# Batched table loads in the edge walks of a graph-attention kernel

## The chip, the cores and the metric

The kernel runs on one core of one Trainium2 chip. The metric is the device time of one execution in microseconds (us), as the median of several runs; lower is better. The profile is one further execution, recorded by the hardware profiler.

## The reference

The kernel computes one block of a graph network over 6250 nodes with 256 features and 200,000 edges sorted by their destination node. Two graph-attention layers come first (four heads of 128 features, then one head of 256), beside a linear-attention mix, and after them a mixture of eight expert networks. What the walks below compute is the attention:

```python
h = (x @ W).reshape(n, heads, out_ch)
logits = leaky_relu(al_s[src] + al_d[dst], 0.2)
m = segment_max(logits, dst)
e = exp(logits - m[dst])
denom = segment_sum(e, dst)
out = segment_sum(h[src] * (e / denom[dst])[:, :, None], dst)
```

For every edge the features of the source node are fetched, weighted, and summed into the destination node. Self loops are added apart from the walks.

## The kernel before, in words

One program runs these stages in order: a first pass (normalised input, `h` for layer 1, and tables over the edges written to HBM), walk 1 (layer 1, `H` = 4 heads in `A` = 2 halves), a finish of layer 1, walk 2 (layer 2, `H` = 1, with the linear-attention mix worked in between), a finish of layer 2, and the experts. Both walks are the same function, `walk_pass` (line 562).

A walk goes over 83 chunks (`CHUNKS`) of ten steps (`CS`), each step two tiles (`TPS`) of 128 edges, so 20 tiles (`CT`) a chunk. The loops over chunks are plain Python loops: every chunk's instructions stand in the program one after the other, and `TURN` with `i`, `r` only numbers slots and semaphore counts. What each engine does in a chunk c:

- POOL (`gather`, L861) issues 20 indirect DMAs that fetch the rows of the source nodes of chunk c into a ring of `RS` chunks (2 in walk 1, 3 in walk 2). Before each step it waits until the same step of the chunk `RS` earlier has been multiplied, and before each chunk until the index table of the chunk is in (`index_in`).
- ACT (`weights` L876 and L878, `scale` L886) takes the exponentials and multiplies three of the four heads' rows by their weights; DVE (`scale`, L1235) does the fourth head in walk 1.
- PE (`multiply`, L1022) sums the weighted rows of a step into at most 128 destination nodes ("a window") by a one-hot matrix `hit`. After step 0 it also runs `spread_targets` for chunk c+1 (L919, twenty small matmuls, which raise `spread_out`); after steps 3 to 6 come four small turns for chunk c+1 (L926, L931, L932, L937, L938, L1007).
- DVE builds `hit` (L1219, from the table `meta`), adds each step's sum into the window's accumulator (L1243 to L1252; the window's number is read into a register by `windows_of`, L713, from the table `win`), and between the steps works out the softmax maxima of chunk c+1: `terms` (L1164 to L1174), `scan_tiles` (L1179, L1180), `scan_ends`, `scan_through` (L1194 to L1200), `gaps` (L1205 to L1214), which raises `gap_ready`, and then `hits_turned` for chunk c+2 (L1160).
- SP only issues DMAs. Its part for chunk c is `follow`, in this order: wait until `gaps` of chunk c is done (this falls at step 6 of chunk c-1), then `load_resets` of chunk c+2 (L775, one DMA for each head, then L777 and L778); wait until all sums of chunk c-1 are added, then `load_tables` of chunk c+2 (`meta` L758, `win` L759) and `load_index` of chunk c+5 (L755); wait for `spread_out` of chunk c+1, then `load_places` of chunk c+2 (L762, 640 KB); then `load_goals` of chunk c+2: wait for its tables (L767), read ten window numbers into registers (L713), and issue ten small DMAs (L770) that PE's `spread_targets` of chunk c+2 waits for.

`index` has six slots (`TS`), `meta` and `win` three (`IS`), `resets` two. Every slot of `index` and of the tables has a semaphore of its own. A slot of `win` is `WROW` = 12 words wide, for ten numbers. At the start of a walk SP loads the index tables of five chunks and the other tables of two, then the places of chunk 0; after a wait for DVE's `cleared` it loads the resets of two chunks and the first goals.

Of the kernel before, what the change touches and what calls it, by code (L numbers as in the profile page):

```python
# [10 lines left out]
ALU = mybir.AluOpType  # L11
# [6 lines left out]
P = 128  # L18
# [23 lines left out]
W = P  # L42
# [4 lines left out]
CS = 10  # L47
CT = CS * TPS
CHUNKS = -(-STEPS // CS)
TURN = 6  # L50
GROUP = 4
CGROUPS = CT // GROUP
BLOCK_ROW = 2 * TPS * P + 2
# [56 lines left out]
def after(engine, sem, n):  # L110

    engine.wait_ge(sem, n + 1)
# [7 lines left out]
def spread(ap, axis, n):  # L120

    shape = list(ap.shape)
    return ap.unsqueeze(axis).to_broadcast(shape[:axis] + [n] + shape[axis:])
# [438 lines left out]
def walk_pass(nc, k, d, layer, H, A, F, attn, acc, table):  # L562
# [3 lines left out]
    HP = H // A  # L566
# [2 lines left out]
    WIDE = OUT + HP  # L569
    RS = 2 if H > 1 else 3  # L570
    TS = 6
    IS = 3
    WROW = -(-CS // 4) * 4
    HA = H - 1 if H > 1 else H
    RK = H * (CT + 1)
    SPREAD = 3 * 2 * H
# [2 lines left out]
    HBUF = 3  # L579
    assert CHUNKS * CS >= STEPS and CHUNKS * CS <= SP  # L580
    assert TURN % RS == 0 and TURN % TS == 0 and TURN % IS == 0 and TURN * CS % PBUF == 0 and TURN * CGROUPS % HBUF == 0
    with ExitStack() as ctx:
        m = Memory(nc, ctx, f"walk{layer}")
        ring = m.sb("ring", [P, RS, CT, A * HALF_ROW])
        index = m.sb("index", [P, TS, CT], I32)
        meta = m.sb("meta", [P, IS, 2, CT])
        win = m.sb("win", [1, IS, WROW], I32)
        hitT = m.sb("hitT", [W, CT * P], BF16)
        target = m.sb("target", [P, NT, 3, 2 * H], BF16)
        goal = m.sb("goal", [P, CS, 3, 2 * H], BF16)  # L590
        resets = m.sb("resets", [RK, 2, 2, P])
# [13 lines left out]
        hit = m.sb("hit", [P, HBUF, GROUP, W])  # L605
# [59 lines left out]
        count = pK[:, 0:W]  # L665
        weight_k = pK[:, W:W + CT]

        index_in = [m.sem(f"index_in{r}") for r in range(TS)]
        tables_in = [m.sem(f"tables_in{r}") for r in range(IS)]
        place_in = m.sem("place_in")  # L670
        goals_in = m.sem("goals_in")
        resets_in = [m.sem("resets_in0"), m.sem("resets_in1")]
# [24 lines left out]
        def loop(body):  # L697

            def run(eng):
                for c in range(CHUNKS):  # L700
                    body(c, c // TURN, c % TURN)

            return run

        def after_this(c, i, r):

            if c == CHUNKS - 1:
                return None
            return (c + 1, i + (r + 1) // TURN, (r + 1) % TURN)

        def windows_of(engine, r):

            return nc.values_load_multi_w_load_instructions(win[0:1, r % IS, 0:CS], engines=[engine], min_val=0, max_val=NW - 1,  # L713
                                                              skip_runtime_bounds_check_because="a group's number is a count over NW - 1 comparisons")[1]
# [10 lines left out]
        def rows_of(i, r):  # L725

            return (i * (TURN // RS) + r // RS + 1) * (16 * CT)

        def resets_of(i, r):

            return (i * (TURN // 2) + r // 2 + 1) * (16 * (H + 2))

        def index_of(i, r):

            return (i * (TURN // TS) + r // TS + 1) * 16

        def tables_of(i, r):

            return (i * (TURN // IS) + r // IS + 1) * 32

# [9 lines left out]
        with nc.Block() as block:  # L750

            @block.sync
            def _(sp):
                def load_index(c, r):
                    sp.dma_start(index[:, r % TS, :], d["index"][:, bass.ds(c * CT, CT)]).then_inc(index_in[r % TS], 16)  # L755

                def load_tables(c, r):
                    sp.dma_start(meta[:, r % IS, :, :], d["meta"][:, :, bass.ds(c * CT, CT)]).then_inc(tables_in[r % IS], 16)  # L758
                    sp.dma_start(win[:, r % IS, 0:CS], d["windows"].unsqueeze(0)[:, bass.ds(c * CS, CS)]).then_inc(tables_in[r % IS], 16)  # L759

                def load_places(n):
                    sp.dma_start(hitT[:, :], d["places"][0:CHUNKS * CS, :].rearrange("(c s) e -> c (s e)", s=CS)[bass.ds(n, 1), :].to_broadcast([W, CT * P])  # L762
                                 ).then_inc(place_in, 16)

                def load_goals(n, i, r):
                    sp.wait_ge(tables_in[r % IS], tables_of(i, r))
                    sp.sem_inc(part_seen, 1)  # L767
                    at = windows_of(mybir.EngineType.SP, r)
                    for s in range(CS):
                        sp.dma_start(goal[:, s, :, :], target[:, at[s], :, :]).then_inc(goals_in, 16)  # L770

                def load_resets(n, r):
                    of = d["resets"].rearrange("s u w e -> (s u) (w e)")
                    for h in range(H):
                        sp.dma_start(resets[h * (CT + 1) + 1:(h + 1) * (CT + 1), r % 2, :, :].rearrange("t w e -> t (w e)"),  # L775
                                     of[bass.ds(n * CT, CT), :]).then_inc(resets_in[r % 2], 16)
                    sp.dma_start(reset0[:, r % 2:r % 2 + 1], of[bass.ds(n * CT, 1), 0:1]).then_inc(resets_in[r % 2], 16)  # L777
                    sp.dma_start(through[:, r % 2, :, :, 1:],  # L778
                                 spread(d["through"].unsqueeze(0)[:, :, bass.ds(n * CT, CT)], 2, H)).then_inc(resets_in[r % 2], 16)
# [20 lines left out]
                def mix_stores(c):  # L800
                    for t in mix_tiles(c - 1):
                        sp.wait_ge(base_ready, t + 1)
                        sp.dma_start(d["base"][t * P:(t + 1) * P, :], xb[:, t % XB, :]).then_inc(base_stored[t % XB], 16)
# [11 lines left out]
                        load_turned(t)  # L815
                        sp.dma_start(xb[:, t % XB, :], d["x"][t * P:(t + 1) * P, :]).then_inc(xb_in[t % XB], 16)

                for c in range(TS - 1):
                    load_index(c, c)
                for c in range(IS - 1):  # L820
                    load_tables(c, c)
                load_places(0)
                sp.wait_ge(cleared, 1)
# [9 lines left out]
                def follow(c, i, r):  # L833
                    after(sp, gap_ready, c + 1)
                    load_resets(c + 2, r)
                    sp.wait_ge(added, c * CS + PBUF)
                    load_tables(c + IS - 1, r + IS - 1)
                    if c + TS - 1 < CHUNKS:
                        load_index(c + TS - 1, r + TS - 1)
                    sp.wait_ge(spread_out, c + 2)  # L840
                    load_places(c + 2)
                    load_goals(c + 2, (c + 2) // TURN, (c + 2) % TURN)
                    if mixing:
                        mix_stores(c)
                        mix_tile_loads(c)
# [7 lines left out]
            @block.gpsimd  # L853
            def _(pool):
                def gather(c, i, r):
                    pool.wait_ge(index_in[r % TS], index_of(i, r))
                    for s in range(CS):
                        pool.wait_ge(multiplied, c * CS + s + 1)
                        pool.sem_inc(index_seen, 1)
                        for t in range(s * TPS, (s + 1) * TPS):  # L860
                            pool.indirect_dma_start(ring[:, r % RS, t, :], None, table,  # L861
                                                    bass.IndirectOffsetOnAxis(ap=index[:, r % TS, t:t + 1], axis=0)).then_inc(rows_in[r % RS], 16)

                loop(gather)(pool)
# [188 lines left out]
            def _(dve):  # L1053
# [149 lines left out]
                def gaps(n, i, r):  # L1203
                    dve.wait_ge(peaks_turned, n + 1)
                    nc.vector.tensor_tensor(pair[:, 1, :, 1:], peak_h[:, :, 1:], dt[:, :, H:].rearrange("p t h -> p h t"), ALU.add)  # L1205
                    nc.vector.tensor_tensor(pair[0:1, 1, :, 0], peak_h[0:1, :, 1], dt[0:1, 0, H:], ALU.add)
                    for a in range(A):
                        nc.vector.tensor_tensor(tail(r, HP * (FH + 1))[:, :, a, :], peak_h[:, a * HP:(a + 1) * HP, 1:].rearrange("p h t -> p t h"),
                                                spread(meta[:, r % IS, 1, :], 2, HP), ALU.mult)
                    dve.drain()  # L1210
                    nc.vector.scalar_tensor_tensor(out=pair[:, :, :, :], in0=pair[:, :, :, :], scalar=SLOPE, in1=pair[:, :, :, :],
                                                   op0=ALU.mult, op1=ALU.max)
                    dve.drain()
                    nc.vector.tensor_tensor(gap[:, :, :], pair[:, 0, :, :], pair[:, 1, :, :], ALU.subtract).then_inc(gap_ready, 1)  # L1214

                def hits(c, i, r, g):
                    dve.wait_ge(tables_in[r % IS], tables_of(i, r))
                    dve.wait_ge(multiplied, c * CS + (g + 1 - HBUF) * (GROUP // TPS) + AHEAD)
                    nc.vector.tensor_tensor(hit[:, (r * CGROUPS + g) % HBUF, :, :], spread(count, 1, GROUP), spread(meta[:, r % IS, 0, g * GROUP:(g + 1) * GROUP], 2, W),  # L1219
                                            ALU.is_equal).then_inc(hits_ready, 1)  # L1220

                def ratios(n, i, r):
# [31 lines left out]
                def chunk(c, i, r):  # L1254
# [32 lines left out]
                    if n:  # L1287
                        gaps(*n)
# [921 lines left out]
```

## Time and profile before

| | us |
|---|---|
| median of 3 runs | 5681.7 |
| lowest, highest run | 5672.57, 5684.13 |
| span of the profiled execution, first to last instruction | 6588.7 |

The profiled execution shows no time of its own beside its span, and the span is 907.0 us (16%) above the median of the runs. What the profile shows of a share or an order must so be carried over with care. Engine shares of the span: PE 71%, POOL 55%, DVE 47%, ACT 43%. Walk 1 takes about 183 to 2830 us of the span, walk 2 about 3008 to 5590 us, and the experts stand behind it. In the rows, SPq is SyncE's queue of DMA issues; "remote" is a wait whose releaser the profile does not name, and "issue" a gap in which the engine waited for nothing that is shown.

### The profile page before, as it was taken

The numbers are of one execution on the slowest core, as the hardware profiler recorded it, in microseconds if no ns is written. First come the engines' busy times: TensorE is split into PE (matmuls) and PEld (weight loads), VectorE is DVE, ScalarE is ACT, GpSimd is POOL, SyncE is SP. The second block draws the span as 40 slices with busy tenths as digits, with TensorE's granted clock in tenths as the row PEclk, the third lists the DMA queues.
The fourth block names the chain that finished last, engine by engine and source line by source line (L and its number), as shares of the span: only waits on it lengthen the run. The fifth ranks groups of instructions, "written<-read, shape, count | busy, mean of one in ns | idle before, by whom it ended". The sixth has DMA issues, their size and how long they took to land. (4 is left out here: it accounts for less than half of the span.)

```text
span 6588.7 us, 83150 instructions
## 1 busy us (share of the span) xinstructions
PE 4647.1 (71%) x21069; PEld 3510.5 (53%) x21069; DVE 3112.7 (47%) x8587; ACT 2835.5 (43%) x8419; POOL 3631.1 (55%) x3778
## 2 busy tenths in 40 slices
PE   7477777777777777773555565665555556699999
PEld 4355555555555555652444444443343444588887
DVE  4365666656656666662444444444444444711111
ACT  2455655655555556673334334333232223322222
POOL 0565666656655666545666666666666664244443
PEclk9698888888888888896777777777777777699999
DMA  5676777777777777633444444444455553644332
GB/s 190 193 203 196 201 200 199 202 195 203 201 196 199 203 197 202 191 116 102 118 115 116 119 114 116 118 115 116 118 136 139 139 135 107 203 157 131 125 133 79
DMA packets 703586, 1027.53 MB, mean 156 GB/s; under 512 B 391738, under 2 KB 483736, under 8 KB 702862
## 3 DMA queue, kind: packets, MB, share of 16 engines
q0 software_dynamic: 229312, 718.64, 39.2%
q1 hardware_dynamic: 473246, 302.52, 15.9%
q8 instruction: 181, 2.97, 0.2%
q14 instruction: 287, 2.35, 0.1%
q10 hardware_dynamic: 560, 1.05, 0.1%
HBM read 951.81 MB, written 65.48 MB: 154 GB/s over the span
## 5 line engine op out<-in xcount | busy, mean ns | idle before, releaser
L861 POOL DMA_INDIRECT walk_ring<-s_h,walk_index x3320 | 3170.3, 955 | 2120.8 <-issue 1004.3
L1022 PE MATMUL walk_pM<-walk_ring,walk_hit 128*128 128x262 f32 (+1 forms) x9960 | 3017.1, 455 | 235.2 <-issue 133.4
L1022 PEld LDWEIGHTS walk_pM<-walk_ring,walk_hit 128*128 128x128 f32 x9960 | 2150.5, 225 | 789.7 <-issue 385.3
L886 ACT ACTIVATE walk_ring<-walk_ring 128x128 f32<-128x128 f32 (+1 forms) x6640 | 2140.9, 414 | 30.2 <-issue 24.3
L1252 DVE TENSOR_TENSOR acc<-walk_pM,acc 128x520 f32 (+1 forms) x1494 | 833.6, 558 | 1834.2 <-remote 1040.8
L876 ACT ACTIVATE walk_ring<-walk_gap 128x40 f32<-128x40 f32 (+1 forms) x249 | 54.0, 258 | 2549.6 <-DVE walk_gap L1214 1867.9
L926 PE MATMUL walk_pC<-all_ident,walk_best 128*84 128x128 f32 (+1 forms) x166 | 57.7, 348 | 857.5 <-DVE walk_best L1170 552.7
L1219 DVE TENSOR_TENSOR walk_hit<-walk_pK,walk_meta 128x512 f32<-128x512 f32 x830 | 560.9, 676 | 11.8
L926 PEld LDWEIGHTS walk_pC<-all_ident,walk_best 128*84 128x84 f32 (+1 forms) x166 | 19.8, 119 | 925.0 <-issue 924.9
L2050 ACT ACTIVATE expert_hT<-expert_pH,expert_b 128x256 f32<-128x256 f32 x448 | 187.6, 470 | 595.2 <-PE expert_pH L2101 595.2
L2101 PE MATMUL expert_pH<-expert_xT,expert_w 128*128 128x256 f32 x1792 | 397.8, 380 | 1.7 <-issue 1.7
L2113 PE MATMUL expert_pO<-down,expert_hT 128*128 x1792 | 395.9, 379 | 0.0
L2101 PEld LDWEIGHTS expert_pH<-expert_xT,expert_w 128*128 128x128 f32 x1792 | 341.5, 191 | 49.0 <-issue 2.3
L2113 PEld LDWEIGHTS expert_pO<-down,expert_hT 128*128 128x128 f32 x1792 | 336.3, 190 | 43.5
L2025 POOL DMA_INDIRECT out_dram<-expert_total,all_token_out x112 | 113.8, 1016 | 313.9 <-DVE expert_total L2067 256.5
L1235 DVE TENSOR_TENSOR walk_ring<-walk_ring,walk_pK 128x512 f32<-128x512 f32 x415 | 279.6, 674 | 0.1
L1007 PE MATMUL walk_pC<-all_ident,walk_back_max 84*128 84x84 f32 (+1 forms) x166 | 45.9, 277 | 302.3 <-DVE walk_back_max L1200 240.2
L1007 PEld LDWEIGHTS walk_pC<-all_ident,walk_back_max 84*128 84x128 f32 (+1 forms) x166 | 28.7, 173 | 361.9 <-issue 358.0
L2058 DVE COPY expert_xT<-expert_pX 128x512 f32<-128x512 f32 x56 | 38.7, 692 | 362.6 <-PE expert_pX L2090 331.7
L2062 DVE TENSOR_TENSOR expert_out<-expert_pO,expert_b 128x256 f32<-128x256 f32 x112 | 47.6, 425 | 293.0 <-PE expert_pO L2113 293.0
L2020 POOL DMA_INDIRECT expert_total<-out_dram,all_token_in x112 | 107.6, 961 | 139.1 <-DMA out_dram<-expert_total,all_token_out 118.1
L2012 POOL DMA_INDIRECT expert_xin<-s_y,all_token_in x112 | 107.5, 959 | 126.5 <-POOLq L99 92.0
(319 smaller groups left out, 4119.1 us busy)
## 6 DMA issues: line engine op xcount, KB each, us to landing
walk_hitT<-s_places SPq DMA_DIRECT2D x166, 640.0 KB
expert_w<-in_fw_dram SPq DMA_DIRECT2D x56, 1024.0 KB
walk_ring<-s_h,walk_index POOLq DMA_INDIRECT x3320
walk_goal<-walk_target SPq DMA_DIRECT2D x830, 6.0 KB
walk_goal<-walk_target SPq DMA_DIRECT2D x830, 1.5 KB
walk_xk<-s_xT SPq DMA_DIRECT2D x98, 128.0 KB
walk_resets<-s_resets SPq DMA_DIRECT2D x415, 20.0 KB
down<-in_fw_dram SPq DMA_DIRECT2D x8, 1024.0 KB, 11.9
```

What stands on the lines that cost most here:

```text
L861: pool.indirect_dma_start(ring[:, r % RS, t, :], None, table, bass.IndirectOffsetOnAxis(ap=index[:, r % TS, t:t + 1], axis=0)).then_inc(ro ...
L886: last = nc.scalar.activation(row, row, ACT.Copy, scale=ring[:, r % RS, t, at + FH:at + FH + 1])
L1022: last = nc.tensor.matmul(pM[:, b, a, 0:WIDE], hit[:, (r * CGROUPS + g) % HBUF, t % GROUP, :], ring[:, r % RS, t, a * HALF_ROW:a * HALF_RO ...
L1219: nc.vector.tensor_tensor(hit[:, (r * CGROUPS + g) % HBUF, :, :], spread(count, 1, GROUP), spread(meta[:, r % IS, 0, g * GROUP:(g + 1) * G ...
L1235: nc.vector.tensor_tensor(rows, rows, spread(weight_k[:, g * GROUP:(g + 1) * GROUP], 2, FH), ALU.mult).then_inc(dve_scaled, 1)
L1252: nc.vector.tensor_tensor(to, pM[:, b, :, 0:OUT], to, ALU.add).then_inc(added, 1)
L2012: pool.indirect_dma_start(xin[:, h % SX, :], None, d["y"], bass.IndirectOffsetOnAxis(ap=k["token_in"][:, h:h + 1], axis=0)).then_inc(x_in[ ...
L2020: pool.indirect_dma_start(total[:, h % 4, :], None, d["out"], bass.IndirectOffsetOnAxis(ap=k["token_in"][:, h:h + 1], axis=0)).then_inc(to ...
L2025: pool.indirect_dma_start(d["out"], bass.IndirectOffsetOnAxis(ap=k["token_out"][:, h:h + 1], axis=0), total[:, h % 4, :], None, bounds_che ...
L2050: nc.scalar.activation(hT[:, t % 2, c, :], pH[:, j, c % HB, :], ACT.Gelu, bias=b1[:, e, c:c + 1]).then_inc(h_ready, 1)
L2101: last = nc.tensor.matmul(pH[:, j, c % HB, :], w1[:, t % WS, kk, c * P:(c + 1) * P], xT[:, t % 2, kk, :], start=(kk == 0), stop=(kk == DK ...
L2113: last = nc.tensor.matmul(pO[:, q, 0:D], hT[:, t % 2, c, q * P:(q + 1) * P], w2[:, e, c, :], start=(c == 0), stop=(c == HC - 1))
```

## The change

Index, `meta` and `win` are fetched for an even chunk and the odd one behind it together (`PAIR` = 2), with one semaphore for a pair; `meta` keeps its two parts apart so that a pair's columns lie side by side, `WROW` is 10, so that a pair of window rows is 20 words in a row, and `IS` is 4. SP runs `load_tables` (now chunks c+2 and c+3) and `load_index` (c+4 and c+5) at even c only. At the start of a walk two pairs of index tables and one pair of the others are fetched. `load_resets` brings the rows of all heads in one DMA, whose source is repeated for each head and begins one row earlier, so that slot 0 of each head is written too; only chunk 0 is loaded as before. `TURN` is 12.

```diff
-TURN = 6
+TURN = 12
-    IS = 3
-    WROW = -(-CS // 4) * 4
+    IS = 4
+    PAIR = 2
+    WROW = CS
-        meta = m.sb("meta", [P, IS, 2, CT])
+        meta = m.sb("meta", [P, 2, IS, CT])
-        index_in = [m.sem(f"index_in{r}") for r in range(TS)]
-        tables_in = [m.sem(f"tables_in{r}") for r in range(IS)]
+        index_in = [m.sem(f"index_in{r}") for r in range(TS // PAIR)]
+        tables_in = [m.sem(f"tables_in{r}") for r in range(IS // PAIR)]
...
                 def load_index(c, r):
-                    sp.dma_start(index[:, r % TS, :], d["index"][:, bass.ds(c * CT, CT)]).then_inc(index_in[r % TS], 16)
+                    both = min(PAIR, CHUNKS - c)
+                    sp.dma_start(index[:, r % TS:r % TS + both, :].rearrange("p c t -> p (c t)"),
+                                 d["index"][:, bass.ds(c * CT, both * CT)]).then_inc(index_ready(r), 16)
 
                 def load_tables(c, r):
-                    sp.dma_start(meta[:, r % IS, :, :], d["meta"][:, :, bass.ds(c * CT, CT)]).then_inc(tables_in[r % IS], 16)
-                    sp.dma_start(win[:, r % IS, 0:CS], d["windows"].unsqueeze(0)[:, bass.ds(c * CS, CS)]).then_inc(tables_in[r % IS], 16)
+                    both = min(PAIR, CHUNKS - c)
+                    sp.dma_start(meta[:, :, r % IS:r % IS + both, :].rearrange("p a c t -> p a (c t)"),
+                                 d["meta"][:, :, bass.ds(c * CT, both * CT)]).then_inc(tables_ready(r), 16)
+                    sp.dma_start(win[:, r % IS:r % IS + both, 0:CS],
+                                 d["windows"].unsqueeze(0)[:, bass.ds(c * CS, both * CS)].rearrange("o (c s) -> o c s", s=CS)
+                                 ).then_inc(tables_ready(r), 16)
...
                 def load_resets(n, r):
                     of = d["resets"].rearrange("s u w e -> (s u) (w e)")
-                    for h in range(H):
-                        sp.dma_start(resets[h * (CT + 1) + 1:(h + 1) * (CT + 1), r % 2, :, :].rearrange("t w e -> t (w e)"),
-                                     of[bass.ds(n * CT, CT), :]).then_inc(resets_in[r % 2], 16)
+                    if n == 0:
+                        for h in range(H):
+                            sp.dma_start(resets[h * (CT + 1) + 1:(h + 1) * (CT + 1), r % 2, :, :].rearrange("t w e -> t (w e)"),
+                                         of[bass.ds(n * CT, CT), :]).then_inc(resets_in[r % 2], 16)
+                    else:
+                        sp.dma_start(resets[:, r % 2, :, :].rearrange("q w e -> q (w e)"),
+                                     of[bass.ds(n * CT - 1, CT + 1), :].unsqueeze(0).to_broadcast([H, CT + 1, 2 * P])).then_inc(resets_in[r % 2], 16)
...
-                for c in range(TS - 1):
+                for c in range(0, TS - PAIR, PAIR):
                     load_index(c, c)
-                for c in range(IS - 1):
+                for c in range(0, IS - PAIR, PAIR):
                     load_tables(c, c)
...
                     sp.wait_ge(added, c * CS + PBUF)
-                    load_tables(c + IS - 1, r + IS - 1)
-                    if c + TS - 1 < CHUNKS:
-                        load_index(c + TS - 1, r + TS - 1)
+                    if c % PAIR == 0:
+                        load_tables(c + IS - PAIR, r + IS - PAIR)
+                        if c + TS - PAIR < CHUNKS:
+                            load_index(c + TS - PAIR, r + TS - PAIR)
```

The waits for index and tables name the pair's semaphore, and the two reads of `meta` (L1208, L1219) follow its new order of parts.

## Rows read from the trace of the kernel before

**Rows 1.** The page's first line: the span.
```profile
span 6588.7 us, 83150 instructions
```

**Rows 2.** Windows view of line L861: stretch, its length, POOL busy (count), PEclk, DMA share, GB/s.
```profile
182.70:2789.50 2606.80, 1579.58 (x1660) 0.86 0.72 199
3008.10:5555.60 2547.50, 1588.82 (x1660) 0.72 0.46 123
```

**Rows 3.** Timeline of POOL in walk 1: start, length, what, idle before.
```profile
1500.44 0.95 POOL L861 DMA_INDIRECT walk_ring<-s_h,walk_index  x1 [0.30 <-issue]
1501.69 0.95 POOL L861 DMA_INDIRECT walk_ring<-s_h,walk_index  x1 [0.30 <-issue]
```

**Rows 4.** Timeline of SP's queue in walk 1, one chunk.
```profile
1506.06 0.59 SPq L758 DMA_DIRECT2D walk_meta<-s_meta  x1
1506.71 0.44 SPq L759 DMA_DIRECT2D walk_win<-s_windows  x1
1507.20 0.36 SPq L755 DMA_DIRECT2D walk_index<-s_index  x1
1511.58 0.33 SPq L762 DMA_DIRECT2D walk_hitT<-s_places  x1
1513.26 10.24 SPq L770 DMA_DIRECT2D walk_goal<-walk_target  x10
1528.30 1.43 SPq L775 DMA_DIRECT2D walk_resets<-s_resets  x4
```

**Rows 5.** Waits of SP's queue, 260 to 2780 us: total us, times, longest.
```profile
SPq L775 <- DVE walk_gap L1214: 349.4, 43, 11.5
SPq L758 <- DVE acc L1252: 238.7, 49, 6.9
SPq L762 <- remote: 235.9, 52, 8.6
SPq L767 <- DMA walk_win<-s_windows: 2.9, 4, 1.0
```

**Rows 6.** Waits of SP's queue, 3120 to 5540 us.
```profile
SPq L762 <- remote: 486.2, 75, 9.4
...
SPq L758 <- DVE acc L1252: 228.6, 52, 8.1
```

**Rows 7.** Timelines of PE, SP, DVE and POOL in one stretch of walk 2.
```profile
4018.95 0.65 PE L919 MATMUL walk_pC<-walk_goal,walk_hitT 128*128 128x6 bf16 x20
...
4026.21 0.33 SPq L762 DMA_DIRECT2D walk_hitT<-s_places  x1
...
4026.39 0.43 DVE L1252 TENSOR_TENSOR acc<-walk_pM,acc 128x258 f32 x1 [4.86 <-remote]
...
4027.03 0.94 POOL L861 DMA_INDIRECT walk_ring<-s_h,walk_index  x1 [3.11 <-remote]
```

**Rows 8.** Waits of PE and DVE, 260 to 2780 us; PE's next L919, timeline.
```profile
PE walk_pC L919 <- issue: 8.2, 13, 1.9
...
DVE walk_best L1170 <- DMA walk_ring<-s_h,walk_index: 7.6, 7, 1.6
...
1533.88 0.65 PE L919 MATMUL walk_pC<-walk_goal,walk_hitT 128*128 128x24 bf16 x20
```

**Rows 9.** DVE's register load, ns min/median/max (tile walk_win); the instruction behind it, timeline.
```profile
L713 DVEq TENSOR_LOAD <-walk_win x166: 1060/1065/1320, 247.0 to 5582.3; - x166
...
1507.82 0.16 DVE L1243 TENSOR_SCALAR walk_rescale<-walk_pM 128x4 f32<-128x4 f32 x1 [0.59 <-PE walk_pM L1022]
```

**Rows 10.** DMA queues, 400 to 2700 us: packets, MB, share of 16 engines.
```profile
q0 software_dynamic: 117318, 396.50, 60.5%
q1 hardware_dynamic: 156135, 60.81, 11.0%
```

**Rows 11.** Timeline of SP's queue at the start of walk 1.
```profile
184.81 0.35 SPq L762 DMA_DIRECT2D walk_hitT<-s_places  x1
186.21 1.61 SPq L775 DMA_DIRECT2D walk_resets<-s_resets  x4
```

More of the change, by code:

```diff
@@ L729, in resets_of, with index_ready, tables_ready @@
         def resets_of(i, r):
-            return (i * (TURN // 2) + r // 2 + 1) * (16 * (H + 2))
+            return (i * (TURN // 2) + r // 2 + 1) * (16 * 3) + (16 * (H - 1) if r % 2 == 0 else 0)
         def index_of(i, r):
             return (i * (TURN // TS) + r // TS + 1) * 16
+        def index_ready(r):
+            return index_in[r % TS // PAIR]
+        def tables_ready(r):
+            return tables_in[r % IS // PAIR]
         def tables_of(i, r):
@@ L765, in load_goals @@
                 def load_goals(n, i, r):
-                    sp.wait_ge(tables_in[r % IS], tables_of(i, r))
+                    sp.wait_ge(tables_ready(r), tables_of(i, r))
                     sp.sem_inc(part_seen, 1)
@@ L855, in gather @@
                 def gather(c, i, r):
-                    pool.wait_ge(index_in[r % TS], index_of(i, r))
+                    pool.wait_ge(index_ready(r), index_of(i, r))
                     for s in range(CS):
@@ L1208, in gaps @@
                         nc.vector.tensor_tensor(tail(r, HP * (FH + 1))[:, :, a, :], peak_h[:, a * HP:(a + 1) * HP, 1:].rearrange("p h t -> p t h"),
-                                                spread(meta[:, r % IS, 1, :], 2, HP), ALU.mult)
+                                                spread(meta[:, 1, r % IS, :], 2, HP), ALU.mult)
                     dve.drain()
@@ L1216, in hits @@
                 def hits(c, i, r, g):
-                    dve.wait_ge(tables_in[r % IS], tables_of(i, r))
+                    dve.wait_ge(tables_ready(r), tables_of(i, r))
                     dve.wait_ge(multiplied, c * CS + (g + 1 - HBUF) * (GROUP // TPS) + AHEAD)
-                    nc.vector.tensor_tensor(hit[:, (r * CGROUPS + g) % HBUF, :, :], spread(count, 1, GROUP), spread(meta[:, r % IS, 0, g * GROUP:(g + 1) * GROUP], 2, W),
+                    nc.vector.tensor_tensor(hit[:, (r * CGROUPS + g) % HBUF, :, :], spread(count, 1, GROUP), spread(meta[:, 0, r % IS, g * GROUP:(g + 1) * GROUP], 2, W),
                                             ALU.is_equal).then_inc(hits_ready, 1)
```

## The prediction

> **What bounds the kernel now.** I looked first at where the gathers stand. All 1660 of walk 1 are issued in 2606.8 us and all 1660 of walk 2 in 2547.5 us [rows 2]: 31.4 and 30.7 us for each of 83 chunks, 5154.3 us together, which is most of the span of 6588.7 us [rows 1]. Both walks take nearly the same time, though walk 2 moves 123 GB/s against 199 and has a quarter of the heads. What they share is the number of gathers. Back to back, these start every 1.25 us (0.95 busy and 0.30 between) [rows 3], so a chunk cannot go below 20 x 1.25 = 25.0 us, and the walks not below 166 x 25.0 = 4150 us.
>
> Next the gap between profile and timed runs. The span is 907.0 us above the median of 5681.7. In the profile, after PE's burst of twenty small matmuls ends at 4019.60, SP (which waits for just that burst), DVE and POOL all start again only at 4026.21, 4026.39 and 4027.03 [rows 7]. A pause of this kind in each chunk, 907.0 / 166 = 5.5 us, would account for the difference if the timed runs lack it. That is an argument and not a measurement. If it holds, the timed walks take 5154.3 - 907.0 = 4247.3 us, or 25.6 us a chunk, 97 us in all above POOL's floor. So I read the timed kernel as one that POOL's issue rate nearly sets.
>
> Then SP, which alone the change touches. In one chunk it issues resets (1.43 us), meta, win and index (0.59, 0.44, 0.36), places (0.33) and goals (10.24) [rows 4]. Between 260 and 2780 us (80 chunks of 31.4) it sits waiting for 349.4 + 238.7 + 235.9 + 2.9 = 826.9 us, or 10.3 us a chunk; what ends the waits is DVE's gap, DVE's sums and `spread_out`, all later work of others [rows 5]. In walk 2 two of these waits alone make 714.8 us over 79 chunks, 9.0 us a chunk [rows 6]. Its most urgent product, the goals, is issued by 1523.50, and PE's next burst is at 1533.88: 10.4 us to spare for the landing. PE's burst waited 8.2 us in all of walk 1's steady part [rows 8]. SP follows; it does not lead.
>
> **The change part by part.**
>
> *Pairs of tables and index on SP.* Before, 0.59 + 0.44 + 0.36 = 1.39 us a chunk [rows 4]. After, one set for two chunks. The trace has no transfer of the new size: if issue time goes by transfers the saving is 0.70 us a chunk, if by bytes it is 0. I take 0.70, since the number of separate pieces (one per partition and part) stays that of a single set. All of it lies between the wait for DVE's sums and the wait for `spread_out`, where SP stands idle afterwards (235.9 us in walk 1, 486.2 in walk 2 [rows 5, 6]); the wait grows by what the issues lose. On the path: 0. The set for an even chunk c+2 is still asked for in the same `follow` in which the goals need it; that wait cost 2.9 us in walk 1 [rows 5], and on odd chunks it goes. Behind it only SP's own goals queue up.
>
> *Resets in one transfer.* Walk 1: four issues, 1.43 us, become one of 84 rows; bounds 0.36 (a quarter of 1.43) to 1.43. I take 0.6, the row of meta, which has the most pieces (0.59), so 0.8 us saved. Walk 2 had one issue already. The saving stands before the wait for DVE's sums (238.7 us [rows 5]) and is lost in it. Resets are read a chunk later. On the path: 0.
>
> If that cover were gone, SP's whole saving would be at most 83 x (0.70 + 1.07) + 83 x 0.70 = 205 us, and POOL's floor would let through 97 us of it.
>
> *Index comes later.* It is now asked for at the start of an even chunk c for c+4. In walk 2 the ring lets the gather of c+4 begin no earlier than chunk c+1, a whole chunk (25 us or more) later; in walk 1, two chunks. POOL's wait stays met: 0. Nothing new is waited for on POOL, and its 1.25 us per gather does not change.
>
> *DMA traffic.* Queue 1's packets took 16 x 2300 x 0.110 / 156135 = 26 ns each, queue 0's 16 x 2300 x 0.605 / 117318 = 190 ns [rows 10]. Index (128) and meta (256) pieces are halved: 192 packets x 26 ns / 16 = 0.3 us a chunk on each engine, between 0 (where POOL sets the pace) and 166 x 0.3 = 50 us. I take 0: the gathers' landing held DVE up 7 times, 7.6 us in all [rows 8]. On the other side, the resets' 84 rows as one transfer may fall on few DMA engines. A 1 KB row lies between 26 ns (390 bytes mean) and 190 ns (3380 bytes mean), by a straight line about 61 ns. Spread over 16 engines it is 5 rows each; on four engines 21 rows, 16 x 61 ns = 1.0 us more on those, at most 83 us over walk 1. I take 0, by the same row, and keep the end for a rival.
>
> The Trainium skill, "DMA: Bandwidth & Descriptors", section "Why a DMA increments its semaphore by 16 and not by 1", says that a transfer runs on the largest number of engines up to 16 that divides the slowest dimension of both sides. By that rule the old transfers of 20 rows use ten engines, and the new one, with 84 rows on one side and four repeats on the other, uses four. The views read here do not separate the engines, so no row shows it; the rule speaks for the unfavourable end above.
>
> *Window rows of 10 words.* Odd slots begin off a 16-byte boundary. DVE's register load takes 1.065 us, and the instruction behind it waited 0.59 us before 1507.82 for PE's sum, not for the load [rows 9]. Bounds 0 to another 1.1 us on odd chunks, 0.59 of it covered here; I take 0, since ten words are read either way. If it were all lost, 83 x 0.5 = 42 us. SP's own load has the goals' slack.
>
> *Start of each walk.* Three index, one meta and one win issue go, about 3 x 0.36 + 0.59 + 0.44 = 2.1 us [rows 4]. In walk 1 SP then waits for DVE's `cleared` from 185.16 to 186.21 anyway [rows 11], so only the second resets count, up to 1.07 us. In walk 2 up to 2.1 us. Bounds 0 to 3.2 us; I take 2.
>
> Sum: 5681.7 - 2 = 5680. Against the profiled execution the same sum is 6588.7 - 2.
>
> **The rivals.**
>
> *Faster: SP leads in the timed runs.* With a chunk at 25.6 us instead of 31.4, 5.8 of SP's 10.3 idle us are gone, and the goals' 10.4 us become some 5. If their landing takes that long, issues taken off SP pull PE's burst ahead, and the DMA relief helps the same way. Against it: what the change removes stands before two waits that others end. Worth up to the 97 us above POOL's floor; the middle, 48 us, gives 5633.
>
> *Slower: resets on few engines.* Gathers are complete only when their slowest DMA engine is. Walk 1's engines are 72% busy in the profile [rows 2]; squeezed from 31.4 to 25.6 us a chunk that is 88%. Four engines with 1.0 us more would be at 92%. If they pace the ring of two chunks in walk 1, the price is 83 x 1.0 = 83 us less 83 x 0.3 = 25 of relief: +58, 5740; if half of it gets through, 5710. It decides once the last gather's landing, and not POOL's issue, releases DVE's `terms`. For it: the utilisation. Against it: only 7.6 us of such waits [rows 8], and POOL itself sits between.
>
> *The change doesn't do what it says:* if SP's issue time goes by bytes, nothing is saved, and the time is 5682, which falls into the first case.
>
> **How the numbers follow.** No change, 5680, own range 5671 to 5690: 0.59. Faster rival: 0.27. Slower rival: 0.14. A measurement of this kernel tells about 0.2% (11 us) from no change, so these are the three chances. The range 5635 to 5705 leaves out the lower half of the faster rival (about 0.12) and a little over half of the slower one (0.07).
>
> **What would show it right or wrong.** SP's issues: L775 in walk 1 near 0.6 us and once a chunk; L758, L759 and L755 83 or so times instead of 166; SP's waits at L758 or L762 longer by what was saved; gathers still 1.25 us apart, and their stretches within 10 us of 2607 and 2547. Walk 1 shorter and walk 2 not would speak for the resets on SP mattering; walk 1 longer, with DVE's L1170 waiting for the ring, for the few engines. The reading of the floor is wrong if the time falls by over 97 us.

## The result, and the profile after

The changed kernel takes 5663.99 us (median of 9 runs, 5655.79 to 5665.52), the kernel before 5676.32 us (9 runs, 5669.93 to 5687.15). The ratio is 0.997, with a 95% interval of 0.996 to 0.9979: about 0.3% faster, 12 us by the medians and 17 us by the ratio. That is in the stated range, but on the other side of the 0.2% that I had set as "no change", and below that case's own range of 5671 to 5690 us. A second timing gave 0.9972 (0.9963 to 0.9981).

The new profile has a span that fits its runs, unlike the one of before [rows 1]. So I took the kernel before once more (experiment 1), and its span then is 5679.1 us. The two clean profiles are compared from here on; "before" without rows means this second one. First the changed kernel: the page's first line and the windows of its gather line (stretch, length, POOL busy, granted clock, DMA share, GB/s; these answer to [rows 1, 2]).

```profile
span 5663.8 us, 82730 instructions
```

```profile
182.10:2319.60 2137.50, 1600.79 (x1660) 0.89 0.84 243
2539.90:4644.70 2104.80, 1599.43 (x1659) 0.77 0.55 149
```

The same of the kernel before, second profile:

```profile
span 5679.1 us, 83150 instructions
```

```profile
181.10:2332.40 2151.30, 1600.00 (x1660) 0.90 0.84 241
2553.00:4657.50 2104.50, 1599.09 (x1660) 0.77 0.56 149
```

Of the 15.3 us between the spans, 13.8 lie in walk 1's gathers; walk 2's stretch differs by 0.3 us. In walk 2 a chunk takes 25.4 us, POOL's floor of 25.0 and a little; in walk 1 it took 25.9 and takes 25.8.

What SP issues in one even and one odd chunk of walk 1 after the change (timeline; answers to [rows 4]):

```profile
1515.33 0.75 SPq L794 DMA_DIRECT2D walk_resets<-s_resets  x1
...
1519.96 0.59 SPq L770 DMA_DIRECT2D walk_meta<-s_meta  x1
1520.59 0.44 SPq L772 DMA_DIRECT2D walk_win<-s_windows  x1
1521.07 0.45 SPq L765 DMA_DIRECT2D walk_index<-s_index  x1
1521.56 0.42 SPq L777 DMA_DIRECT2D walk_hitT<-s_places  x1
1525.64 6.74 SPq L785 DMA_DIRECT2D walk_goal<-walk_target  x10
1542.19 0.76 SPq L794 DMA_DIRECT2D walk_resets<-s_resets  x1
...
1548.08 0.35 SPq L777 DMA_DIRECT2D walk_hitT<-s_places  x1
```

A pair's transfers issue in the time of a single set, and the odd chunk has none. The resets take 0.75 us where they took 1.43.

Where the walks now wait, kernel before, second profile, 240 to 2310 us (total us, times, longest; answers to [rows 8]):

```profile
PE walk_pC L926 <- DVE walk_best L1170: 283.6, 73, 5.6
DVE walk_best L1170 <- DMA walk_ring<-s_h,walk_index: 248.3, 79, 4.9
...
POOL walk_ring L861 <- PE walk_pM L1022: 102.9, 252, 2.0
```

The changed kernel, same stretch:

```profile
PE walk_pC L946 <- DVE walk_best L1190: 279.7, 78, 5.6
...
DVE walk_best L1190 <- DMA walk_ring<-s_h,walk_index: 199.0, 79, 5.0
POOL walk_ring L881 <- PE walk_pM L1042: 88.8, 247, 2.0
```

The chain of waits is this. In every chunk DVE's `terms` waits for the last gathers of the next chunk to land, 3.1 us each time (248.3 / 79), 2.5 after the change. PE's first turn waits for DVE, its later steps stand behind the turn, and POOL, whose ring is two chunks deep in walk 1, waits for these steps. In the first profile the row of DVE's wait read 7.6 us in 7 times [rows 8]; all engines paused there, for a reason that the profile does not name.

The traces bear this chain out chunk by chunk. Call landing time the stretch from the start of a chunk's last gather on POOL to the start of DVE's `terms`, which waits for it: 5.96 us on average over 80 chunks of walk 1 in the kernel before. In the chunks above the median of it, POOL stood idle 0.97 us (beyond its usual 0.30 between gathers) in the fifth to seventh step of its next chunk; behind the other chunks it was 0.19 us. In the remaining steps POOL hardly waits at all (under 0.01 us a step on average).

SP's queue was not idle where I had seen it idle. Its waits before the change, second profile, 240 to 2310 us (answers to [rows 5]):

```profile
SPq L775 <- DVE walk_gap L1214: 773.5, 80, 15.0
SPq L758 <- DVE acc L1252: 169.2, 80, 2.5
SPq L767 <- DMA walk_win<-s_windows: 151.0, 80, 3.8
SPq L762 <- PE walk_pC L919: 0.4, 2, 0.2
```

The wait for `spread_out` was 235.9 us in the first profile and is 0.4 here, so SP goes from the tables straight to the places, and then waits 1.9 us a chunk for the tables to land. Index, `meta`, `win` and places are all asked for within 2 us at the chunk's start, just ahead of the next chunk's last gather, which lands 8 to 10 us behind them:

```profile
1499.67 0.61 SPq L758 DMA_DIRECT2D walk_meta<-s_meta  x1
1500.32 0.44 SPq L759 DMA_DIRECT2D walk_win<-s_windows  x1
1500.81 0.35 SPq L755 DMA_DIRECT2D walk_index<-s_index  x1
1501.20 0.42 SPq L762 DMA_DIRECT2D walk_hitT<-s_places  x1
...
1504.02 0.95 POOL L861 DMA_INDIRECT walk_ring<-s_h,walk_index  x1 [0.30 <-issue]
...
1509.32 0.38 DVE L1170 TENSOR_TENSOR walk_best<-walk_ring,walk_dt 128x40 f32<-128x40 f32 x2 [2.88 <-DMA walk_ring<-s_h,walk_index]
```

Moments within a chunk are given below as distances from the end of DVE's `gaps` (averages over walk 1). In the kernel before, SP issues `meta` at 4.7 us, index at 5.8 and the places at 6.3; POOL starts the last gather at 8.6, and DVE starts `terms` at 14.6.

### The profile page after: what moved, and what is told of

It is laid out like the page before. It is cut to its first block and busy times, and to the rows that moved or that the text cites. A ratio compares the mean times of both kernels' runs of the same rounds, so it can differ in the third digit from the quotient of the medians.

```text
span 5663.8 us, 82730 instructions
## 1 busy us (share of the span) xinstructions
PE 4356.2 (77%) x21069; PEld 3348.9 (59%) x21069; DVE 3077.8 (54%) x8587; ACT 2830.1 (50%) x8419; POOL 3662.8 (65%) x3778
## 5 line engine op out<-in xcount | busy, mean ns | idle before, releaser
L1042 PE MATMUL walk_pM<-walk_ring,walk_hit 128*128 128x262 f32 (+1 forms) x9960 | 2795.1, 433 | 29.2 <-DVE acc L1270 17.9
L1042 PEld LDWEIGHTS walk_pM<-walk_ring,walk_hit 128*128 128x128 f32 x9960 | 2035.9, 213 | 454.1 <-issue 73.5
L1190 DVE TENSOR_TENSOR walk_best<-walk_ring,walk_dt 128x40 f32<-128x40 f32 (+1 forms) x249 | 47.1, 217 | 784.4 <-DMA walk_ring<-s_h,walk_index 784.3
L1459 POOL TENSOR_TENSOR finish_own<-finish_own,finish_bias 128x512 f32<-128x512 f32 x49 | 82.5, 1685 | 120.5 <-ACT finish_own L1517 120.5
```

Of the source, the lines that this page charges most:

```text
L1042: last = nc.tensor.matmul(pM[:, b, a, 0:WIDE], hit[:, (r * CGROUPS + g) % HBUF, t % GROUP, :], ring[:, r % RS, t, a * HALF_ROW:a * HALF_RO ...
```

## The experiments

The first four ran on one chip beside 35 runs of the kernel before (5683.02 us).

A length of walk 1's gathers is that of one profiled execution, and these differ: the one of experiment 10 took 16 us less than the median of its runs, that of 5 took 14 less, those of 4, 6 and 8 took 7 to 9 less, and that of 7 took 7 more; the others lie within 4 us. The table at the end of this section has them beside each other.

**1. The kernel before, again.** No edit.

> The kernel before, unchanged, as a control and for a second profile. Every theory: 5676 us, ratio 1.000 (0.999 to 1.001). If the profile's span is near 5677 us instead of 6589, the pauses in the first profile (5.5 us a chunk) belonged to that one execution, and the walks' gathers should then stand near 25.6 to 25.9 us a chunk in both walks; if the span is near 6589 again, they belong to the profiling of this program.

Measured: 5682.68 us, ratio 1.0007 (0.9997 to 1.0017), span 5679.1 us. The pauses belonged to that one execution. The walks' chunks take 25.9 and 25.4 us; I had worked out 25.6 for both.

**2. Resets in one transfer, alone.**

The edit of `load_resets` and `resets_of` is that of the change, chunk 0 as before.

```diff
-                    for h in range(H):
-                        sp.dma_start(resets[h * (CT + 1) + 1:(h + 1) * (CT + 1), r % 2, :, :].rearrange("t w e -> t (w e)"),
-                                     of[bass.ds(n * CT, CT), :]).then_inc(resets_in[r % 2], 16)
...
```

> The kernel before with the resets of all heads in one transfer, and nothing else. Theory A (fewer small packets, from index and meta, let walk 1's gathers land earlier): same, 5676 us, since the rows of the resets are as many as before. Theory B (SP's issue time: 1.43 us of resets and 1.39 us of tables stand ahead of the places and goals): about half of the change's 12 us, 5670. Theory C (the 84 rows fall on four DMA engines, which hold the gathers back): slower, 5680 to 5700, and the pairs then gain more than 12 us alone.

Measured: 5681.06 us, ratio 0.9999 (0.999 to 1.0009), walk 1's gathers in 2152.2 us. Nothing gained and nothing lost: theories B and C both fall for this part. SP waits longer for DVE's sums instead, 215.5 us against 169.2, and issues `meta` and the places when it did before.

```profile
SPq L758 <- DVE acc L1256: 215.5, 80, 3.1
```

The page of this kernel and that of before count the packets:

```profile
DMA packets 700796, 1027.92 MB, mean 181 GB/s; under 512 B 388540, under 2 KB 480948, under 8 KB 700074
```

```profile
DMA packets 703587, 1027.53 MB, mean 181 GB/s; under 512 B 391739, under 2 KB 483737, under 8 KB 702863
```

2791 fewer. The Trainium skill, "DMA: Bandwidth & Descriptors", section "Why a DMA increments its semaphore by 16 and not by 1", says that each engine used ends with one write of its own to the semaphore. By its rule for the number of engines these are ten for 20 rows, four for 84 rows against four repeats, and seven for 21. Counting that write as one packet, 82 loads in walk 1 have 4 x (20 + 10) before and 84 + 4 after, 32 fewer; in walk 2, 30 before and 21 + 7 after, 2 fewer: 82 x 34 = 2788. The trace agrees with the rule, and in its parts too: there are 410 more packets of 1 KB (82 x 5 rows) and 3198 fewer of 4 bytes (82 x 39 writes). So the count fits four engines for the resets of walk 1, and this costs nothing that can be measured.

**3. Index in pairs, alone.**

```diff
-                    if c + TS - 1 < CHUNKS:
-                        load_index(c + TS - 1, r + TS - 1)
+                    if c % PAIR == 0 and c + TS - PAIR < CHUNKS:
+                        load_index(c + TS - PAIR, r + TS - PAIR)
```

> The kernel before with the index tables fetched for two chunks at a time, and nothing else. Theory A: a third of the small packets go (64 of 192 a chunk), 4 us faster, 5672. Theory B: 0.18 us of SP's time a chunk, 1 us, 5675. Theory D (only the start of the walks gains, by transfers not issued ahead of the first gathers and goals): 1 to 2 us, and the spacing of gathers in the steady part stays.

Measured: 5664.54 us, ratio 0.9966 (0.9956 to 0.9977), walk 1's gathers in 2140.8 us.

**4. `meta` and `win` in pairs, alone.**

```diff
                     sp.wait_ge(added, c * CS + PBUF)
-                    load_tables(c + IS - 1, r + IS - 1)
+                    if c % PAIR == 0:
+                        load_tables(c + IS - PAIR, r + IS - PAIR)
```

> The kernel before with meta and window numbers fetched for two chunks at a time (four slots, ten words a window row), and nothing else. Theory A: two thirds of the small packets go (128 of 192 a chunk), 8 us faster, 5668. Theory B: 0.5 us of SP's time a chunk, 2 to 3 us, 5673. Theory D: 1 us.

Measured: 5669.07 us, ratio 0.9974 (0.9963 to 0.9985), 2139.3 us. Each half gives what the whole change gives; the parts do not add up. None of the four theories had said that. It speaks against a price per packet over the whole walk and for something at one moment. The next experiments ask what stands in the way there: the small pieces on the DMA engines, or SP's issue time ahead of the places.

Experiments 5 to 8 ran on one chip, the kernel before at 5691.69 us (15 runs).

**5. Nothing in pairs, all moved to step 6 of the chunk before.** Four slots, ten words.

```diff
                     load_resets(c + 2, r)
+                    load_tables(c + 2, r + 2)
+                    if c + TS - 1 < CHUNKS:
+                        load_index(c + TS - 1, r + TS - 1)
                     sp.wait_ge(added, c * CS + PBUF)
-                    load_tables(c + IS - 1, r + IS - 1)
-                    if c + TS - 1 < CHUNKS:
-                        load_index(c + TS - 1, r + TS - 1)
```

> The kernel before, with meta, window numbers and index still fetched for every chunk one by one (as many transfers and pieces as before; four slots of ten words so that a slot is free), but issued with the resets, at step 6 of the chunk before, ahead of the wait for DVE's sums. Theory M (what costs is that these transfers are issued at the chunk's start, where the last gathers of the next chunk land, whether by their pieces or by SP's 1.4 us ahead of the places): faster than the change, 5650 to 5665, with even and odd chunks alike. Theory N (the number of pieces over the whole walk): no gain, 5680.

Measured: 5668.74 us, ratio 0.996 (0.9946 to 0.9974), and 2126.7 us for walk 1's gathers, the shortest of all (in an execution that was itself 14 us under the median). With every transfer still made singly, the gain is there. Theory N falls. The move is a small one: `meta` is now issued at 2.6 us instead of 4.7, and the places at 5.9 instead of 6.3. Even and odd chunks became more alike, not fully (see the last section).

**6. The same, with index in pairs.** Edit of experiment 5 with `load_index` as in experiment 3.

> As the moved kernel, and the index tables in pairs besides. Theory M: as the moved kernel within 3 us, since nothing of it stands at the chunk's start any more. Theory N: 5 to 10 us faster than the moved kernel.

Measured: 5666.02 us, ratio 0.9954 (0.994 to 0.9967), 2.7 us from experiment 5, far inside both intervals; 2130.6 us for walk 1's gathers. As theory M has it.

**7. SP's issue time put back, without the pieces.** On the changed kernel, walk 1; `spare` is a stretch that nothing reads.

```diff
+                    elif H > 1:
+                        if c > 1:
+                            sp.wait_ge(spare_in, (c // 2) * 48)
+                        for q in range(3):
+                            sp.dma_start(spare[1:2, q * CS:(q + 1) * CS], d["through"][0:1, bass.ds(c * CS, CS)]).then_inc(spare_in, 16)
```

> The changed kernel, and in walk 1 three transfers of a single 40-byte piece each at every odd chunk, where the tables and the index used to be issued: SP's 1.2 us ahead of the places come back, the pieces don't (3 for 385). They write a spare stretch that nothing reads. Theory S (SP's time ahead of the places): the gain is gone, 5675 to 5680, and odd chunks take 25 us or more again. Theory P (the pieces beside the landing gathers): the gain stays, 5664, odd chunks near 24.3 us.

Measured: 5672.15 us, ratio 0.9963 (0.9949 to 0.9976), walk 1's gathers in 2144.4 us. The gain stays. But the experiment does less than its heading says: on odd chunks of the changed kernel SP waits 3.9 us each time (156.4 / 40) for DVE's sums and then `spread_out`, the three issues vanish in that wait, and the places are still issued at 5.9 us, as in the changed kernel. So theory S is not put to the test here. The most it could claim is the 0.3 us by which the places moved; what speaks against it are experiments 9 and 10.

**8. The pieces put back behind the places.** On the changed kernel, walk 1, odd chunks.

```diff
                     load_places(c + 2)
+                    if c % PAIR == 1 and H > 1:
+                        if c > 1:
+                            sp.wait_ge(spare_in, (c // 2) * 48)
+                        for q in range(3):
+                            sp.dma_start(spare[64:128, q * 2 * CT:(q + 1) * 2 * CT].rearrange("p (a t) -> p a t", a=2),
+                                         d["meta"][64:128, :, bass.ds((c + q) * CT, CT)]).then_inc(spare_in, 16)
```

> The changed kernel, and in walk 1 at every odd chunk three transfers of 128 pieces of 80 bytes right behind the places: the pieces come back at nearly the moment they had, while the places keep their early start (the goals are issued 1.2 us or more later instead). They write a spare stretch that nothing reads. Theory S: the gain stays, 5664. Theory P: the gain is gone or mostly gone, 5672 to 5680.

Measured: 5679.34 us, ratio 0.9981 (0.9971 to 0.9991). By its ratio it is between the two expectations, about 0.1% of the 0.3% lost; the interval overlaps that of experiment 7, though on this one chip its runs are slower by 6 us on average (an interval of about 1 to 12 us). Walk 1's gathers took 2141.2 us against 2144.4 there, in executions 9 us under and 7 us above their medians. The goals are issued 2.2 us later on odd chunks (11.0 us for 8.8); PE's burst, which needs them, waits for them in neither kernel. It leans to theory P and does not settle it. So the dose was raised on the kernel before. The last four ran on one chip, the kernel before at 5677.53 us (20 runs).

**9 and 10. 384 more pieces in every chunk of walk 1, at two moments.** The same block, in 9 right behind `load_places`, at 6.8 us, in 10 right behind `load_resets`, at 2.6 us:

```diff
+                    if H > 1:
+                        if c > 0:
+                            sp.wait_ge(spare_in, c * 48)
+                        for q in range(3):
+                            sp.dma_start(spare[64:128, q * 2 * CT:(q + 1) * 2 * CT].rearrange("p (a t) -> p a t", a=2),
+                                         d["meta"][64:128, :, bass.ds(c * CT, CT)]).then_inc(spare_in, 16)
```

> The kernel before, and in walk 1 at every chunk three more transfers of 128 pieces of 80 bytes each right behind the places (384 pieces, as many as index and meta have); they write a spare stretch that nothing reads. Theory P (pieces beside the landing of the last gathers): slower by about what taking them off at half the chunks gave, times two or less: 5695 to 5720 where the kernel before has 5683, and DVE waits longer for the gathers than 248 us. Theory S (SP's time ahead of the places, untouched here): 5683.

> The same 384 extra pieces a chunk in walk 1 on the kernel before, but issued behind the resets, at step 6 of the chunk. If the moment counts: the same time as the kernel before within 0.1%. If the number of pieces counts wherever they stand: slower, as with the extra pieces at the chunk's start.

Measured: at the start 5704.96 us, ratio 1.0051 (1.0037 to 1.0064); at step 6, 5673.22 us, ratio 0.999 (0.9981 to 0.9999). The same pieces cost 27 us at one moment and nothing 4 us earlier. The window of walk 1's gathers, and then the waits of DVE and POOL in 240 to 2310 us, first for experiment 9:

```profile
178.60:2362.30 2183.70, 1601.12 (x1660) 0.90 0.83 239
```

```profile
DVE walk_best L1178 <- DMA walk_ring<-s_h,walk_index: 264.6, 78, 5.3
POOL walk_ring L869 <- PE walk_pM L1030: 137.4, 286, 2.0
```

and for experiment 10:

```profile
178.70:2312.70 2134.00, 1601.22 (x1659) 0.91 0.85 245
```

```profile
DVE walk_best L1178 <- DMA walk_ring<-s_h,walk_index: 250.4, 80, 4.8
POOL walk_ring L869 <- PE walk_pM L1030: 80.2, 230, 2.0
```

Walk 1 is 32.4 us longer than before in 9 and 17.3 us shorter in 10. The shortening in 10 is mostly that of the one execution that was profiled (5657.23 us, 16 us under the median); by the timed runs 10 is at most a little faster than the kernel before. DVE's total wait does not follow it either (250.4 us for 248.3); the landing time does, 5.74 us against 5.96, and 6.32 in 9. In both, `meta`, index and places are issued within 0.1 us of when the kernel before issues them. The goals come 0.3 to 0.4 us later in 9, but between 240 and 2310 us PE's burst waits for goals in none of the profiles of experiments 1 to 12. So neither SP's time ahead of the places nor late goals make the difference between 9 and 10.

**11 and 12. The changed kernel and the moved one, on one chip.** Edits as they stand above.

> The changed kernel once more, unaltered, on the same chip as the moved one: ratio 0.997 (0.996 to 0.998). It gives the difference between the two without a change of chip.

> The kernel with all loads still one by one but issued at step 6, once more. If the moment is the whole of the gain: at or a little below the changed kernel, ratio 0.995 to 0.997. If the fewer pieces of the changed kernel add to it: above the changed kernel.

Measured: 5663.52 us, ratio 0.9972 (0.9963 to 0.9981), walk 1's gathers in 2141.8 us, and 5652.88 us, ratio 0.9958 (0.9945 to 0.9972). Here, and by the ratios of experiment 5 and the first timing of the change, moving was ahead of pairing by 0.1%, with intervals that overlap; that it is better is likely and not shown. Experiment 12's window and waits:

```profile
178.80:2306.00 2127.20, 1603.40 (x1660) 0.91 0.84 244
```

```profile
DVE walk_best L1170 <- DMA walk_ring<-s_h,walk_index: 212.7, 80, 5.0
POOL walk_ring L861 <- PE walk_pM L1022: 72.3, 228, 1.1
```

POOL's wait for PE follows the length of walk 1 over these profiles: 137.4, 102.9, 88.8, 80.2, 72.3 us of wait for 2183.7, 2151.3, 2137.5, 2134.0 and 2127.2 us. And so, roughly, does the landing time (averages over 80 chunks of walk 1, from the traces):

| kernel | profiled execution, us | walk 1's gathers, us | landing time, us |
|---|---|---|---|
| 9, pieces added behind the places | 5704.96 | 2183.7 | 6.32 |
| 2, resets alone | 5677.52 | 2152.2 | 6.04 |
| before, second profile | 5680.79 | 2151.3 | 5.96 |
| 7, tiny issues | 5678.85 | 2144.4 | 5.56 |
| changed, second profile (11) | 5665.31 | 2141.8 | 5.70 |
| 8, pieces back on odd chunks | 5670.81 | 2141.2 | 5.80 |
| 3, index in pairs | 5665.56 | 2140.8 | 5.60 |
| 4, tables in pairs | 5661.96 | 2139.3 | 5.50 |
| changed, first profile | 5665.52 | 2137.5 | 5.57 |
| 10, pieces added behind the resets | 5657.23 | 2134.0 | 5.74 |
| 6, moved, index in pairs | 5657.75 | 2130.6 | 5.55 |
| 12, moved | 5652.88 | 2127.2 | 5.31 |
| 5, moved | 5655.10 | 2126.7 | 5.29 |

How the pieces lengthen it is not separated. In experiment 9 they run on the DMA engines from 10 to 14 us, while the last gather is under way, and the places' packets no later than before (median 9.9 us against 10.0): that points to the pieces themselves. In the kernel before nearly all pieces are through by 8.3 us, before the last gather starts, and the places' 640 KB, which stand behind them in the same queue, run next to it; the places' median falls from 10.0 us to 9.0 in the changed kernel and to 8.7 in the moved one. So the gain of the change may come from the pieces, from the places that run earlier without them, or from both.

## Why the prediction was right and where it was wrong

- *POOL's issue rate nearly sets the pace; the profile's extra 907.0 us are pauses.* Right, and shown: spacing of 1.25 us, 4255.8 us for both stretches where 4247.3 was worked out. Of the 106 us above the floor of 4150, 76 lie in walk 1 and 30 in walk 2.
- *SP's savings end in waits.* Right in result: the resets' 0.7 us a chunk gave nothing (experiment 2), and issue time put back vanished in a wait (7). SP's waits for DVE's sums and `spread_out` grew from 169.6 to 262.6 us in 240 to 2310 us. The evidence was partly wrong: the slack at `spread_out` was not there before the change.
- *DMA traffic, taken at 0 of 0 to 50 us.* This is the step that failed. I held that the gathers' landing delays nobody, by the row of 7.6 us [rows 8]. In the clean profile that wait is 248.3 us in 79 chunks, and POOL stands idle where the landing was late (0.97 us a chunk against 0.19). With fewer pieces issued ahead of the last gather, the landing time fell from 5.96 to 5.57 us and walk 1 by 14 us. The term was also put wrongly: I priced packets by their number (0.3 us a chunk), while the same number costs 27 us or nothing by its moment (9, 10). And I took 26 ns for a piece, the mean of a queue that also carries the places' packets of 5 KB (230 ns each in the second profile); the pieces of 80 bytes took 12 ns.
- *The rival "SP leads"* has its result, a faster kernel, for another reason than its own; experiments 2, 9 and 10 speak against its mechanism. It did name the DMA relief as a help. *The rival "resets on few engines"* had its mechanism (four engines, by the packet count) and no price.
- *Window rows of ten words, taken at 0 of 0 to 1.1 us.* The load did get slower, by more than the bound; see below.
- *Start of the walks, 2 us.* Not seen: walk 1's first gather stands at 182.1 us after and 181.1 before, and between the walks 220.3 us lie after and 220.6 before.
- *The signs.* SP issues the resets in 0.75 us and `meta`, `win` and index 84 times each, and gathers stand 1.25 us apart, as forecast; their stretches are far from 2607 and 2547 us, which were the first profile's. Walk 1 shorter and walk 2 not was to speak for the resets on SP; it happened, and experiment 2 shows that the resets gave nothing.

The time was in the range, but not by the sum: the case it rests on, no change, missed by 7 us, and the range held because it took in half of the faster rival. 5.4 of the 18 us between 5681.7 and the result are only the kernel before, whose median over more runs is 5676.32.

The error behind the failed step is one of reading. I had noted that all engines paused in the profile, and had carried the pauses off the total, but not off the rows of waits. With pauses of all engines between a transfer's issue and its use, every transfer looks early.

What stays open: why a part of the pieces (a third of what the change takes off in experiment 3, two thirds in 4) gives all of the gain, and whether the pieces or the places behind them are what the last gather meets.

## What to carry to other kernels

Small loads with slack of their own can still delay a large transfer that has none; issue them where nothing urgent is landing, before thinking of making them fewer. Here the same loads, issued 2 us earlier in a chunk of 26 and not merged, gave at least as much as the merging. A profile is one execution: set its own time beside the median of the runs before a difference of 10 us is read from it. And where a profile's span is far above the timed runs, take it again before any wait in it is read as slack.

## What the runs showed that was not expected

Window rows of ten words make the register load slow at every second slot. The loads of the kernel before and of the changed one (ns min/median/max; answers to [rows 9]):

```profile
L713 DVEq TENSOR_LOAD <-walk_win x166: 1060/1065/1327, 218.6 to 4671.1; - x166
```

```profile
L714 SPq TENSOR_LOAD <-walk_win x166: 1102/1286/2327, 189.9 to 4610.2; - x166
L714 DVEq TENSOR_LOAD <-walk_win x166: 1060/1218/2324, 220.7 to 4658.2; - x166
```

By slot the medians on DVE in walk 1 are 1073, 2286, 1073 and 2285 ns: rows that begin at 40 or 120 bytes take twice as long as those at 0 or 80, on SP too (2248 against 1119). Experiments 4, 5, 6 and 12 have it, experiment 3 with twelve words a row does not (median 1066). On DVE it shows as a wait before the first sum of each odd chunk in walk 1 of the changed kernel:

```profile
1495.27 0.16 DVE L1263 TENSOR_SCALAR walk_rescale<-walk_pM 128x4 f32<-128x4 f32 x1 [0.67 <-issue]
1521.04 0.15 DVE L1263 TENSOR_SCALAR walk_rescale<-walk_pM 128x4 f32<-128x4 f32 x1
1548.66 0.16 DVE L1263 TENSOR_SCALAR walk_rescale<-walk_pM 128x4 f32<-128x4 f32 x1 [0.67 <-issue]
```

These waits come to 28.0 us in 40 times, and what the slow loads cost in all was not tried. They also shift the first sums themselves, so that from these starts one chunk takes 25.77 us and the next 27.62. Measured clear of them, from one end of DVE's `gaps` to the next, the stretch with an even chunk's start takes 26.6 us in the changed kernel and the one with an odd chunk's 25.0. In experiment 3, which has no slow loads, it is still 26.4 and 25.2; in experiment 12, which has them but treats all chunks alike, 25.6 and 25.6 (25.9 and 25.3 in experiment 5). So most of this alternation goes with the loads that odd chunks lack, and not with the slow register loads.
